# Splitting the first parameter load and moving the context loads to ScalarE's queue

## The reference

```
query  = ctx @ Wq.T + bq                      # 4 x 256 x 128
key    = ctx @ Wk.T + bk                      # 4 x 256 x 128
attention = softmax(query @ key.T, axis=-1)   # 4 x 256 x 256
x = x + tanh(g_xattn) * (layernorm(x) . attention.T)
h = fp8(layernorm(x))
y = fp8(gelu(h @ w_gating[0]) * (h @ w_gating[1])) @ fp8(w_linear)
x = x + tanh(g_ffn) * y
```

## Time and profile before

| | us |
|---|---|
| median of 3 runs | 49.64 |
| lowest and highest | 49.51 and 49.75 |
| the profiled execution | 49.62 |
| its span, first to last instruction | 47.8 |
| TensorE busy | 42.3 (88%) |
| VectorE busy | 33.6 (70%) |
| ScalarE busy | 27.9 (58%) |
| GpSimd busy | 22.2 (46%) |

### The profile page before, as it was taken

One profiled execution on the slowest core, in us unless ns is written; L12 is line 12 of the kernel. 1 busy time (PEld: TensorE's weight loads), 2 busy tenths in 40 slices (PEclk: granted clock), 3 DMA queues, 4 the chain that ended last, 5 costly groups with the idle time before them and its releaser, 6 DMA issues.

```text
span 47.8 us, 861 instructions
## 1 busy us (share of the span) xinstructions
PE 42.3 (88%) x246; PEld 28.6 (60%) x246; DVE 33.6 (70%) x107; ACT 27.9 (58%) x63; POOL 22.2 (46%) x48
## 2 busy tenths in 40 slices
PE   3998999999999789999989999999999999998000
PEld 1317788877878377865226655565645888884000
DVE  0101629856999998839999999187669977999600
ACT  0901866997889904084549876964448495363000
POOL 3200495484988897810049249980000069700500
PEclk9999999999999999999999999999999999999999
DMA  0499999999999972000000000000000002450092
GB/s 0 70 369 382 341 385 375 368 123 109 105 104 60 81 71 19 14 0 0 0 7 0 0 0 0 0 0 0 0 7 0 0 14 86 168 185 0 7 338 101
DMA packets 3461, 4.65 MB, mean 97 GB/s; under 512 B 384, under 2 KB 2176, under 8 KB 3456
## 3 DMA queue, kind: packets, MB, share of 16 engines
q1 hardware_dynamic: 2304, 3.48, 20.7%
q0 software_dynamic: 864, 0.79, 18.7%
q10 hardware_dynamic: 288, 0.33, 1.9%
HBM read 5.90 MB, written 1.05 MB: 145 GB/s over the span
## 4 chain that ended last, share of the span: by engine, by line
PE 58%; DVE 13%; ACT 9%; DMA 6%; issue 5%; DVEq 2%; POOL 1%; POOLq 0%
PE bank L702 11%; PE bank L631 9%; PE bank L683 8%; PE bank L677 8%; PE bank L596 7%; DMA par<-params_ctxT 6%; PE bank L580 5%; DVE ap L495 4%; PE bank L588 4%; PE bank L603 3%; ACT L404 3%; DVE x L466 3%; DVE st L471 2%; ACT attnT L358 2%; ACT e L352 2%
## 5 line engine op out<-in xcount | busy, mean ns | idle before, releaser
L378 ACT ACTIVATE gl<-bank 128x512 bf16<-128x512 f32 (+1 forms) x20 | 10.2, 510 | 6.4 <-PE bank L677 5.9
L495 DVE SCALAR_TENSOR_TENSOR ap<-bank,gl 128x512 f16<-128x512 f32 (+1 forms) x20 | 11.6, 581 | 3.3 <-PE bank L683 1.8
L683 PE MATMUL bank<-xq,wg 128*128 128x512 fp8e4 (+1 forms) x40 | 10.2, 337 | 0.2 <-DVE ap L495 0.2
L677 PE MATMUL bank<-xq,wg 128*128 128x512 fp8e4 (+1 forms) x40 | 10.2, 337 | 0.0
L702 PE MATMUL bank<-wl,aq 128*128 128x256 fp8e4 x64 | 9.6, 273 | 0.0
L631 PE MATMUL bank<-attnT,xT_sb 128*128 128x256 f32 x32 | 8.5, 393 | 0.5 <-ACT attnT L358 0.5
L702 PEld LDWEIGHTS bank<-wl,aq 128*128 128x128 f16 x64 | 6.2, 98 | 2.4 <-DVE aq L504 0.2
L631 PEld LDWEIGHTS bank<-attnT,xT_sb 128*128 128x128 f32 x32 | 5.4, 190 | 1.9 <-ACT attnT L358 1.5
L683 PEld LDWEIGHTS bank<-xq,wg 128*128 128x128 fp8e4 x40 | 3.6, 98 | 3.9 <-DVE ap L495 1.4
L504 DVE TENSOR_SCALAR aq<-ap 128x512 uint16<-128x512 uint16 (+1 forms) x20 | 5.9, 298 | 0.0
L285 POOL TENSOR_TENSOR r<-ve,neg_half 128x2 f32<-128x2 f32 x4 | 3.2, 788 | 5.9 <-DVE ve L478 5.9
(11 more groups left out here) (50 smaller groups left out, 55.6 us busy)
## 6 DMA issues: line engine op xcount, KB each, us to landing
x_sb<-x SPq DMA_DIRECT2D x4, 256.0 KB, 4.9
xT_sb<-xT SPq DMA_DIRECT2D x4, 256.0 KB, 5.5
out<-yo SPq DMA_DIRECT2D x5, 128.0 KB, 1.7
wg<-w_gating POOLq DMA_DIRECT2D x4, 128.0 KB, 7.6
par<-params_ctxT SPq DMA_DIRECT2D x1, 256.0 KB, 3.4
wl<-w_linear POOLq DMA_DIRECT2D x2, 128.0 KB, 6.1
out<-yo SPq DMA_DIRECT2D x1, 256.0 KB, 2.2
par<-params_ctxT SPq DMA_DIRECT2D x1, 194.0 KB, 3.0
```

Of the source, the lines that this page charges most:

```text
L378: nc.scalar.activation(gl[:, s % 2, toks], gate_b[s % 2][:, toks], ACT.Gelu_apprx_tanh).then_inc(gelu_ready, 1)
L495: nc.vector.scalar_tensor_tensor(ap[:, s % NAP, toks], up_b[s % 2][:, toks], ACT_SCALE, gl[:, s % 2, toks], ALU.mult, ALU.mult).then_inc(p ...
L677: mm = nc.tensor.matmul(gate_b[s % 2][:, toks], wg8[:, c, k, 0, o:o + P], xq[:, g, k, toks], start=(k == 0), stop=(k == KC - 1))
L683: mm = nc.tensor.matmul(up_b[s % 2][:, toks], wg8[:, c, k, 1, o:o + P], xq[:, g, k, toks], start=(k == 0), stop=(k == KC - 1))
```

## The change

The array is cut in four pieces. SyncE issues piece 0, which is now the query weight, biases and gates alone (132 columns, 66 KB), and then goes on to x. ScalarE issues three pieces: context 0 (256 columns, 128 KB), key weight and context 1 (384 columns, 192 KB), contexts 2 and 3 (512 columns, 256 KB). The first query projection waits for pieces 0 and 1, the first key projection for piece 2, the query projections of items 2 and 3 for piece 3.

```diff
-    CUTS = (0, P + 4 + L, NPAR + 2 * L, NPAR + 4 * L)
+    CUTS = (0, P + 4, P + 4 + L, NPAR + 2 * L, NPAR + 4 * L)
 ...
         def _(sp):
-            for c in (0, 2):
-                cols = slice(CUTS[c], CUTS[c + 1])
-                sp.dma_start(par[:, cols], params_ctxT[:, cols]).then_inc(s_ctx[c], 16)
+            cols = slice(CUTS[0], CUTS[1])
+            sp.dma_start(par[:, cols], params_ctxT[:, cols]).then_inc(s_ctx[0], 16)
 ...
         def _(act):
-            cols = slice(CUTS[1], CUTS[2])
-            act.dma_start(par[:, cols], params_ctxT[:, cols]).then_inc(s_ctx[1], 16)
+            for c in (1, 2, 3):
+                cols = slice(CUTS[c], CUTS[c + 1])
+                act.dma_start(par[:, cols], params_ctxT[:, cols]).then_inc(s_ctx[c], 16)
             act.wait_ge(s_ctx[0], 16)
 ...
             def project_q(b):
-                if b != 1:
-                    pe.wait_ge(s_ctx[min(b, 2)], 16)
+                if b == 0:
+                    pe.wait_ge(s_ctx[0], 16)
+                    pe.wait_ge(s_ctx[1], 16)
+                if b >= 2:
+                    pe.wait_ge(s_ctx[3], 16)
 ...
             def project_k(b):
                 if b == 0:
-                    pe.wait_ge(s_ctx[1], 16)
+                    pe.wait_ge(s_ctx[2], 16)
```

## The result

The changed kernel takes 50.53 us (median of 4 runs, 50.02 to 52.77), the kernel before 49.58 beside it (4 runs): a ratio of 1.0188, interval 1.0106 to 1.0271.

A forecast was written before the change was run, and what follows sets the result against it. The prediction took the first par DMA, then TensorE's unbroken projections and energies, as the bound. The key projection starting 0.20 later was its only term: 49.62 + 0.20 = 49.82 us, range 49.5 to 50.2.

The forecast's parts named there:

- Key piece: Second load on ScalarE's queue, in turn with x: lands at 4.8, key matmul at 4.94 instead of 4.74, path 0.20 later.
- Contexts 2 and 3: Third load on ScalarE's queue: lands at 6.2 instead of about 4.6, with 0.5 us of cover before project_q(2).
- The clock: TensorE's longer idle at 4.7 may keep it at 1.2 GHz longer, each matmul pair so done costing 0.43 more.
- second rival: ScalarE's queue lies some 0.5 us back: key piece at 5.3, project_k(0) 0.7 later; 49.95 to 50.3, middle 50.1, chance 0.24.
- The base of the sum: The profiled kernel before: key matmul at 4.74, time 49.62, to which the forecast added 0.20.
- Context 0: First load on ScalarE's queue, awaited by the first query projection: lands at 3.65, query starts at 3.69 instead of 3.73.
- the state at 2.5 us: Packets moved by 2.5 us in the kernel before, SyncE's queue 62 and ScalarE's 10, used to forecast the landings.
- ScalarE's extra issues: Two more DMA issues, 0.41 us each, push ScalarE's table load from 1.17 to 2.0; cost nothing, cover 1.4 us.
- VectorE's earlier statistics: x of item 0 lands at 4.4 instead of 5.2, VectorE's statistics come 0.8 us earlier, outside the chain: worth nothing.
- the third rival: GpSimd's weight loads, issued 0.8 us earlier, delay x of item 3 and VectorE's residual by some 0.2: 50.0, chance 0.06.
- the first (faster): Context 0 lands by 3.45, key piece by 4.3, key projection at 4.53 to 4.6: 49.42 to 49.48, chance 0.18.
- the rule of whole packets: DMA engines drain 9 to 17 descriptors before switching queues: context 0 at 4.1, key piece at 5.3, time about 50.3.

The follow-up runs named there:

- e7: The kernel before, with project_k(0) also waiting for x of item 0, no load moved: 51.00 us (50.55 to 52.91, 6 runs), ratio 1.0251.
- e8: The changed kernel with ten warm-up matmuls and not six: 50.35 us (50.01 to 51.35, 6 runs), ratio 1.0192.
- e3: The kernel before with only contexts 2 and 3 moved, to ScalarE's second load: 49.46 us (49.13 to 50.25, 12 runs), ratio 0.9994.
- e9: The changed kernel with key weight and context 1 second on SyncE's queue, ahead of x: 50.25 us (49.87 to 51.74, 6 runs), ratio 1.0154.
- e1: The changed kernel again, no edit: median 51.97 us (49.86 to 52.42, 6 runs), before 49.66; the trace is of a run of 52.42.
- e2: The changed kernel with contexts 2 and 3 back on SyncE, ahead of x: 50.14 us (49.59 to 54.27, 12 runs), ratio 1.0108.

## Why the prediction was wrong

The direction and the path were right and the number was too small: 49.82 with a range to 50.2 against 50.53. The profiled execution, 50.02, lies inside the range, but that is luck: it is the fastest of the four.

The step that failed is the sum. It has a single term, 0.20 for a key piece that lands at 4.80, and puts contexts 2 and 3 and the clock at nothing.

**Key piece.** Forecast 4.8; landings of 4.95, 5.29 and about 4.66 in three traces of the changed kernel. The term was taken as one value where it moves by 0.6. What I added behind the landing was right: from landing to the end of the key's pair I had 0.74 (4.80 to 4.94, and 0.60 as from 4.74 to 5.34 in the earlier trace rows), and 4.95 to 5.69 is 0.74. So the 0.35 of the profiled execution is my 0.20 and the 0.15 by which the landing was later. At 5.29 the same working gives 0.69.

**Contexts 2 and 3.** Forecast 6.2 with 0.5 us of cover, worth nothing. They landed at 7.0, 7.2 and 7.7: the cover was gone, and in one of three traces their wait is the whole shift, 0.43. What failed is the share: behind the key piece I counted 1.31 us for 256 KB with as much of x. From 4.5 to 6.6 us, in the changed kernel's first trace, SyncE's queue moved 0.50 MB and ScalarE's 0.23, so they got a third of the bytes and not half.

**The clock.** I named it in the second rival as an aside and gave it no size of its own in the sum. The remark that the gap "may keep it at 1.2 GHz longer" is what seven of 16 runs show by their times, at 2.10 us in the one that was traced. e7 has such runs in the kernel before without a load moved, e8 has none with all loads moved; with the table I count it as shown that the pause matters, not how the chip decides, nor which runs it strikes. It is not the whole miss: without the run at 52.77 the median of the first four would be 50.30, still above the range.

**The base of the sum.** The 0.20 was the distance to a key matmul at 4.74, in one execution in which the clock rose at 4.74; with the clock up early it stands at 4.36 (e3). A kernel that does not wait can gain from an early clock, and the changed one, which waits for a load, cannot. That is argued and not shown: no second trace of the kernel before exists, and its profiled time, 49.62, lies near the median of its 66 runs, 49.7, so the base explains little of the median.

**What stays open.** The nine runs of the changed kernel without a late clock have their median at 50.30, some 0.6 above before (49.7). Two of them are traced, at 0.40 and 0.47 above the profiled execution of before. The key piece at 5.29, contexts 2 and 3, and a clock that rises a microsecond late as in e9 could each give the rest; no run tells the shares.

**Context 0.** Forecast 3.65, with the query within 0.1 of 3.7. It landed by 3.3 and the query started at 3.41. What failed is the state at 2.5 us. I carried over the 10 packets of ScalarE's queue and the 62 of SyncE's; they were 73 and 128. ScalarE's queue was not late by itself: its first packet moved at 1.8, 0.1 behind SyncE's, and before at 2.2, 0.5 behind. The count of x, 52 rows by 3.32, was near (0.13 MB by 3.3 is some 60). The earlier query gained nothing, as the prediction said of it; it only lengthened the pause.

**The second rival.** The landing past 5.0 and the matmuls at half speed are its signs, and both were seen in e1. Its mechanism, a queue of ScalarE that lies 0.5 us back, was not. Its "half of that gives 0.45" is no half of 0.7 (that would be 0.35, for 49.97) but the middle between 0.20 and 0.7; its range ends at 50.3.

**Right.** ScalarE's extra issues, VectorE's earlier statistics and GpSimd's earlier issue cost nothing, though x of item 0 landed at 4.76 and not at 4.4. x of item 3 landed at 11.0 and not at 10.3, and VectorE took its statistics at 13.84 without a wait, 0.35 later like all of the chain, so the third rival did not occur; nor did the first (faster). The case that the prediction worked out beside the rule of whole packets (the Trainium skill, page "DMA: Bandwidth & Descriptors", section "Queues, rings and completion order") had context 0 at 4.1; it landed at 3.3, before most of x had moved, so these runs do not test the rule there. Its 5.3 for the key piece is within the spread of landings, and its time of 50.3 was nearer than mine, if for another reason.

## What to carry to other kernels

Where a first stage waits for several loads, order them by when each is needed, and put nothing in turn with the last one that is still awaited: a load on another queue takes its share of the same DMA engines (from 3.3 to 4.0 us x moved 0.14 MB beside 0.13 of the key piece), and without it the key piece landed after 2.5 us and not 3.8. Give the loads behind the awaited one a price too. While TensorE's clock is still at its lower level, a pause of half a microsecond can cost two, as in e2; here a stage that started 0.3 us earlier and then waited was worse than one that started later and ran through. And ask what the execution in the profile may have owed to chance (here the time at which the clock rose) before a difference of 0.4% is built on it.

## What was unexpected in the hardware

The granted clock column read 1.00 over stretches in which matmuls ran at 1.2 GHz, up to 9.7 us. Kernels whose TensorE does the same in its first microseconds, but for 0.1 us in the start of the query, saw the clock rise at different times: at 4.4 us matmuls ran at 1.2 GHz before (the query's second, 0.43 from 4.31 to 4.74) and at 2.4 GHz in e3 (the key's pair, 0.43 from 4.36 to 4.79). The first 256 KB load of SyncE moved hardly a row before 2.5 us though issued at 1.16, 0.43 after the one ahead of it. And the software queue's loads, issued at 5.07 instead of 5.49, moved their first packet at 9.1 instead of 9.2. SyncE's queue was still busy there in both (82% to 88% from 9.0 to 9.4); that it held them back is not shown.
